# Adaptive-conditioning attention and mixture-of-experts layer: dense units laid into the last batch's head loop, one router for two batches

## What is computed

```python
x = x + attn(wkv(x, f, f, w, u, cond), Wqkv, Wproj)       # 16 heads of 16, q.k scaled by 4
x = x + ffn(wkv(x, f, f, w2, u2, cond))                   # w2, u2: the second pair

# wkv: num and den are two linear recurrences along the tokens, once forwards, once backwards
base = sigmoid(r) * num / max(den, 1e-8);  out = base * (0.8 + 0.2 * tf)

# ffn: 64 experts of width 64 in 8 groups, the 4 best groups, then the 6 best experts of them
h = relu(x @ w1.T) ** 2 * w_dense        # all experts, for all tokens, weighted by the router (mostly 0)
out = h @ w2.T + relu2(x @ shared_up.T) @ shared_down.T
```

## Time and profile before

| | us |
|---|---|
| median of 3 runs (404.63 to 407.39) | 406.7 |
| the profiled execution, its own time | 407.77 |
| its span, first to last instruction | 405.9 |
| PE busy | 317.9 (78%) |
| DVE busy | 322.0 (79%) |
| ACT busy | 201.4 (50%) |
| POOL busy | 126.4 (31%) |
| DMA queue, share of its 16 engines | 50.4% |

### The profile page before, as it was taken

The page is one execution under the profiler, slowest core; times in us unless marked ns, Lnnn a source line. Parts: engine busy times, 40 slices in busy tenths (PEclk is TensorE's granted clock), DMA queues, the critical chain, the costliest instruction groups (busy, mean ns, idle before and its releaser), DMA issues.

```text
span 405.9 us, 6016 instructions
## 1 busy us (share of the span) xinstructions
PE 317.9 (78%) x1552; PEld 245.0 (60%) x1552; DVE 322.0 (79%) x625; ACT 201.4 (50%) x373; POOL 126.4 (31%) x116
## 2 busy tenths in 40 slices
PE   0042378378858887877897897999999999999994
PEld 0031256165737565555665675888888888888882
DVE  6989888966897475686567995888888988888883
ACT  4131406162625264366555564666666666666651
POOL 1519424162050001001222342334334334334331
PEclk9999559658965896896999998999999999999999
DMA  5965907801760176300543544556655566666531
GB/s 174 169 166 151 155 6 185 129 0 56 155 107 3 52 159 103 106 10 8 170 137 131 154 167 156 140 201 186 189 190 192 183 196 190 192 185 190 194 140 52
DMA packets 33055, 55.09 MB, mean 136 GB/s; under 512 B 5207, under 2 KB 13831, under 8 KB 32011
## 3 DMA queue, kind: packets, MB, share of 16 engines
q1 hardware_dynamic: 33034, 54.85, 50.4%
HBM read 47.55 MB, written 5.52 MB: 131 GB/s over the span
## 4 chain that ended last, share of the span: by engine, by line
PE 48%; DVE 13%; issue 3%; ACT 3%; DMA 2%; POOL 1%; DVEq 0%; SPq 0%; ACTq 0%
PE ps L1256 7%; PE ps L1258 7%; PE ps L1257 6%; PE ps L1267 6%; PE ps L1268 6%; PE ps L1269 6%; PE ps L1171 3%; DVE q_st L959 2%; DVE scan L1052 2%; DVE mx L806 2%; PE ps L1139 2%; DMA k_st<-qk_split 2%; DVE qk_lo L1057 1%; PE ps L1158 1%; PE ps L1128 1%
## 5 line engine op out<-in xcount | busy, mean ns | idle before, releaser
L457 POOL TENSOR_TENSOR scan<-scan 128x512 f32<-128x512 f32 x68 | 73.3, 1078 | 137.8 <-ACT scan L584 136.1
L1057 DVE TENSOR_TENSOR qk_lo<-scan,qk_hi 128x512 fp32r<-128x512 f32 x68 | 69.3, 1019 | 31.7 <-ACT qk_hi L591 31.7
L584 ACT ACTIVATE scan<-ps 128x512 f32<-128x512 f32 x68 | 40.7, 599 | 50.2 <-PE ps L1258 50.0
L1267 PE MATMUL ps<-qk_hi,k_st 128*128 128x512 f32 x136 | 54.5, 401 | 4.5 <-DVE qk_lo L1057 4.3
L1256 PE MATMUL ps<-hid_hi,k_st 128*128 128x512 f32 x136 | 54.6, 401 | 2.0 <-DVE q_st L959 2.0
L577 ACT ACTIVATE k_st<-clip 128x512 fp32r<-128x512 f32 x68 | 42.8, 631 | 24.8 <-PE ps L1269 24.8
L1139 PE MATMUL ps<-k_st,q_st 96*128 96x256 f32 x128 | 34.8, 395 | 25.9 <-DMA k_st<-qk_split 22.6
L1258 PE MATMUL ps<-hid_hi,q_st 128*128 128x512 f32 x136 | 54.1, 398 | 0.0
L1257 PE MATMUL ps<-hid_lo,k_st 128*128 128x512 f32 x136 | 53.9, 396 | 0.0
L1268 PE MATMUL ps<-qk_lo,k_st 128*128 128x512 f32 x136 | 53.5, 393 | 0.0
L1269 PE MATMUL ps<-qk_hi,q_st 128*128 128x512 f32 x136 | 53.5, 393 | 0.0
(11 more groups left out here) (118 smaller groups left out, 461.8 us busy)
## 6 DMA issues: line engine op xcount, KB each, us to landing
clip<-in_tiles SPq DMA_DIRECT2D x68, 256.0 KB, 3.0
ex<-gates SPq DMA_DIRECT2D x136, 128.0 KB, 2.9
q_st<-qk_split SPq DMA_DIRECT2D x16, 256.0 KB, 4.8
k_st<-qk_split SPq DMA_DIRECT2D x32, 128.0 KB, 5.6
qk_split<-qk_hi SPq DMA_DIRECT2D x8, 256.0 KB, 2.2
qk_split<-qk_lo SPq DMA_DIRECT2D x8, 256.0 KB, 2.2
f_sb<-in_fT SPq DMA_DIRECT2D x4, 256.0 KB, 10.5
x_sb<-in_xT SPq DMA_DIRECT2D x4, 256.0 KB, 9.7
```

What stands on the lines that cost most here:

```text
L457: g.tensor_tensor(sq[:, k], relu[:, k], relu[:, k], ALU.mult).then_inc(sq_ready, 1)
L1057: TT(act_lo[:, k], act[:, k], act_hi[:, k].bitcast(F32), ALU.subtract).then_inc(act_lo_ready, 1)
L1267: mm(acc, w_hi, act_hi[:, k], start=first, stop=False, skip_group_check=True)
```

## The change

Batch 1's tail is done first, beside the first heads of batch 2. From the second half of batch 2 on there is one loop of 42 slots, s = 0 to 41, on every engine. Slot s holds the shifted scores of one head (batch 2's heads 8 to 15 in slots 0 to 7, batch 3's heads 0 to 7 in slots 9 to 16 and 8 to 15 in slots 18 to 25), the scores of batch 3's head s (slots 0 to 15), and from s=4 on the dense unit n = s-4. The tails of batches 2 and 3 stand in slots 9 to 14 and 27 to 32.

The router handles two batches (512 tokens) at once: 42 steps on tiles twice as wide where the two could be joined, and four small instructions instead of two where they could not. `router(0)` stands alone in slots 0 to 3, six pieces in each; `router(1)` in slots 33 to 36, six pieces in each, beside units. `turn_weights(0)` is in slot 4 before `up(0)`, `turn_weights(1)` in slot 37. On SP the four first weight tiles are loaded before `load_rows(2, 1)`, and `load_rows(3, 0)` and `load_rows(3, 1)` stand behind `load_unit(8)` and `load_unit(16)`.

To make banks free, scores of batch 3 have one PSUM bank instead of two, so do the shifted scores from batch 2's head 8 on, and units 0 to 11 have one bank for `up`. The stacked slot 2 isn't shared with the units' weights any more; the room comes from several buffers that now lie in others (`ekv` in `clip`, `o_ch` in `o_tok`, the router's in `scan` and `num1`). `products` therefore waits for a fourth exponential instead of the third.

```diff
-HEAD = 18
+RT = 2 * QT
+FIRST = 4
+ALONE = 12
+HEAD = NT + RING
@@ banks
         def bank_s(n):
-            return ps[:, n % 2, :].rearrange("p (t k) -> p t k", t=QT)
+            return ps[:, n % 2 if n < H * (B - 1) else 0, :].rearrange("p (t k) -> p t k", t=QT)
 
         def bank_t(n):
-            return ps[:, 2 + n % 2, :].rearrange("p (t q) -> p t q", t=QT)
+            return ps[:, 2 + n % 2 if n < H * (B - 1) - HB else 2, :].rearrange("p (t q) -> p t q", t=QT)
+        def unit_bank(n):
+            return n % 2 if n >= ALONE else 1
@@ SP
+            for b in range(B - 1):
                 load_rows(b, 0)
+                store_qk(b + 1)
+                for w in range(2):
+                    load_stack(w, b + 1, 0)
+                if b == B - 2:
                     sp.wait_ge(ex_ready, 4 * B)
                     sp.wait_ge(esum_ready, 4 * B)
+                    sp.wait_ge(bwd_ready, 8 * B)
                     for n in range(RING):
                         load_raw(n, n)
                 load_rows(b, 1)
+                for w in range(2):
+                    load_stack(w, b + 1, 1)
...
             store_gates(0)
+            for n in range(SHARED, RING):
+                load_spread(0, n, n)
+            for n in range(RING, 9):
+                load_unit(n, 0, n, n % RING)
+            load_rows(B - 1, 0)
+            for n in range(9, 17):
+                load_unit(n, 0, n, n % RING)
+            load_rows(B - 1, 1)
+            for n in range(17, NT):
+                load_unit(n, 0, n, n % RING)
@@ DVE
+            route_now = router(0)
+            for s in range(HEAD + FIRST):
+                n = s - FIRST
+                if s < H:
+                    maximum(3, s)
+                if s < FIRST:
+                    for _ in range(6):
+                        next(route_now, None)
+                if s == FIRST:
+                    route_now = router(1)
+                if s == 8:
+                    low_max(3, 0)
...
+                if s > 32:
+                    for _ in range(6):
+                        next(route_now, None)
+                if n >= 0:
+                    if n > 0:
+                        low_act(n - 1, (n - 1) % 2)
+                    gated(n, n % 2, n % RING, n // RING + 1)
+                    split_lo(n + 2, (n + 2) % RING)
@@ PE
+            for s in range(HEAD + FIRST):
+                n = s - FIRST
+                if s < HB:
+                    shifted_scores(2, HB + s)
+                if HB < s <= 2 * HB:
+                    shifted_scores(3, s - HB - 1)
+                if 2 * HB + 2 <= s < 3 * HB + 2:
+                    shifted_scores(3, s - HB - 2)
+                if s < H:
+                    scores(3, s)
...
+                if s == 4:
+                    turn_weights(0)
...
+                if s == 37:
+                    turn_weights(1)
...
+                if n >= 0:
+                    up(n, n // NT, n % 2, n % RING)
+                if n >= 2:
+                    down(n - 2, (n - 2) // NT, n % 2, (n - 2) % RING, first=(n - 2) % NT == 0, final=n - 2 == NT - 1)
```

More of the change, by code:

```diff
@@ L583, in rectify @@
                     sc.wait_ge(sq_ready, n - 1)
-                a.activation(relu[:, k], bank_h(k), ACT.Relu).then_inc(relu_ready, 1)
+                bank = unit_bank(n) if isinstance(n, int) else k
+                a.activation(relu[:, k], bank_h(bank), ACT.Relu).then_inc(relu_ready, 1)
             def round_act(n, k):
@@ L601, in _ @@
             exponentials(2)
-            for b in range(B):
+            for b in range(2):
                 if b > 0:
@@ new lines, in _ @@
+            low_max(2, 0)
+            maximum(2, HB)
+            maximum(2, HB + 1)
+            normalise(1)
+            maximum(2, HB + 2)
+            maximum(2, HB + 3)
+            split_qk(3, 0)
+            residual(1)
+            maximum(2, HB + 4)
+            maximum(2, HB + 5)
+            split_qk(3, 1)
+            maximum(2, HB + 6)
+            maximum(2, HB + 7)
+            hidden2(1)
+            low_max(2, 1)
+            add_v_bias(3)
+            for n in range(2):
+                split_lo(n, n)
@@ L1310, in _ @@
                 values(b, 1)
-                if b > 1:
-                    turn_weights(b - 2)
-            for h in range(HB + 2, H):
-                shifted_scores(B - 1, h)
-            values(B - 1, 2)
-            values(B - 1, 3)
-            pe.wait_ge(hid_lo_ready, 2)
-            pe.wait_ge(hid_hi_ready, 2)
-            pe.wait_ge(max_ready, H * B)
-            up(0, 0, 0, 0)
-            turn_out(B - 1)
-            up(1, 0, 1, 1)
-            turn_normalised(B - 1)
-            for n in range(2, HEAD):
-                up(n, 0, n % 2, n % RING)
-                if n == 2:
-                    project_out(B - 1)
-                    turn_weights(B - 2)
-                if n == 6:
-                    gate(B - 1)
-                if n == 14:
-                    turn_weights(B - 1)
-                down(n - 2, 0, n % 2, (n - 2) % RING, first=(n == 2))
@@ L1335, in _ @@
-            with pe.Fori(0, (NT - HEAD) // RING) as i:
+            for h in range(HB):
+                shifted_scores(1, HB + h)
+                if h + 2 < HB:
+                    scores(2, h + 2)
+                if h == 4:
+                    values(1, 2)
+                if h == HB - 2:
+                    turn_max(2, 0)
+                    scores(2, HB)
+                    scores(2, HB + 1)
+            values(1, 3)
+            turn_out(1)
+            scores(2, HB + 2)
+            scores(2, HB + 3)
@@ new lines, in _ @@
+            shifted_scores(2, 0)
+            shifted_scores(2, 1)
+            turn_normalised(1)
+            project(3, "q")
+            shifted_scores(2, 2)
+            shifted_scores(2, 3)
+            project_out(1)
+            scores(2, HB + 4)
+            scores(2, HB + 5)
+            project(3, "k")
+            shifted_scores(2, 4)
+            shifted_scores(2, 5)
+            scores(2, HB + 6)
+            scores(2, HB + 7)
+            shifted_scores(2, 6)
+            turn_max(2, 1)
```

592 lines of the change are left out of this document (318 added, 274 removed).

## The result

The changed kernel takes 423.77 us in the median of 4 runs (421.34 to 426.89), beside 406.76 us for the kernel before in the same series: 1.0432 times as long, 95% interval 1.0353 to 1.0511. So the change costs 17 us, where the prediction had 419.0 us, in a range of 405 to 432. The profiled execution took 424.21 us and has a span of 422.4 us, 4.4 more than the 418.0 forecast.

The account below looks back on a forecast made before the run. PE's streaming was taken as the bound. Unit 0 at 172.9 us + 105.2 units + 22.2 other PE work + 25.7 stalls = 326.0 for unit 38; plus 80.3 and 11.7, span 418.0; time 419 us, range 405 to 432.

Parts of the forecast that it names:

- Step 1, the operand: Before unit 0: batch 3's stacked operand lands at 155.1 us, 0.6 us later than in the kernel before.
- Step 1, the rows behind four tiles: Slot 0: the rows of maxima queue behind four weight tiles and land at 159.7 us, 4.0 + 0.6 behind the operand.
- Step 2: Slots 0 to 3: four maxima and all of router(0), 10.4 us, on DVE; unit 0 at 172.9 us, 22.1 sooner.
- Step 3: PE's work from unit 0 to unit 38: 105.2 us of units plus 22.2 of heads, tails and transposes.
- Step 4: PE's stalls from unit 0 to 38, 25.7 us: rows 5.2 and 1.5, tails 2 and 3, router 9.0, clock 5.0.
- Router(1): Slots 33 to 36: DVE needs 19.6 us beside 11.1 of PE, so PE waits 9.0 us (bounds 5 and 17).
- The clock: PE at half clock after three pauses (slots 0 to 3, 9, 37): 5.0 us lost (bounds 0 and 20).
- DVE beside POOL: Second router: DVE slowed by POOL's squares, 2 us counted; the skill's rule alone would add 4.2.
- A: Rival: queue order costs nothing, no waits in slots 0, 9, 18, clock stays up; about 401 us; chance 0.08.
- B: Rival, no change: half of the stalls are in PE's shadow; about 408 us; chance 0.12.
- C: Rival: shared slots run at half clock or bound by hops, +19, 437 us; chance 0.20 together with serialised routers.
- D: Rival: two routers serialise instead of overlapping, at twice a single one each 431 us; chance 0.20 together with half-clock slots.

Follow-up runs that it names:

- experiment 3: The changed kernel with a buffer of its own for `ekv`, so `products` waits for the third exponential again: 421.05 us, ratio 1.0388.
- experiment 4: The kernel before with `products` waiting for the fourth exponential instead of the third: 407.83 us, ratio 1.0078.
- experiment 1: The changed kernel with both `load_rows` of batch 3 issued one unit earlier on SP: 416.65 us, ratio 1.0259.
- experiment 2: The changed kernel with the four first weight tiles issued behind `load_rows(2, 1)` instead of ahead of it: 420.27 us, ratio 1.0366.
- experiment 6: The changed kernel with its routers cut short (no choice of groups and experts, no normalisation): 410.36 us, ratio 1.0171.
- experiment 12: The changed kernel with rows sooner, weight tiles later and `ekv` on its own, a second run of that same kernel: 411.74 us, ratio 1.0094.
- experiment 7: The kernel before with its four routers cut short (no choice of groups and experts, no normalisation): 397.15 us, ratio 0.9834.
- Experiment 10: The changed kernel with rows sooner, tiles later, `ekv` on its own, and also `t_hi` and `t_lo` allocated first: 411.02 us, ratio 1.0097.
- experiment 9: The changed kernel with rows sooner, tiles later, `ekv` on its own, and also its routers cut short: 399.36 us, ratio 0.9865.

## Why the prediction was right, and where its steps were not

The time was 4.8 us above the forecast, and slower was the likely side. The model, unit 0's start plus PE's work plus PE's stalls, held. That the 38 units came within 2.0 us of their sum is in part luck: PE's idle time in them is 14.5 us, where the sum has 20.7, and against that stand half clock, up to 4 us more than forecast, and the pace of the units, 1.3 more. By steps:

**Step 1, the operand: the step that failed.** Forecast 155.1 us, landed at 159.74. Two terms. First, batch 2's loop began 2.7 us later than before (123.91 us against 121.20). Part of this is the later start of `products`, which I had counted at nothing, "DVE scans the other recurrence first": experiments 3 and 4 price it at 1.6 to 3.2 us. Another 0.54 are in that execution's first scan already (9.28 us, before 8.74), and are absent from the profiles of experiments 1, 2 and 6, which have the same front end. How the rest divides can't be told from one profile, as this start varies by 2.4 us between two executions of one program (experiment 12); experiments 1, 2 and 6 have it at 121.8 to 122.2. Second, `evacuate_qk(3, 1)` was to be 0.6 us later for `second_exp(1)`, and was 2.65 us later on top of the above. The chain of after, in that place:

```profile
146.16 0.44 DVE ex L899
146.62 0.63 ACT ex L557
147.25 0.12 ACT den L559
147.68 0.61 ACT ex L561
148.29 0.73 ACT qk_hi L520 x2
149.05 0.89 DVE qk_lo L839 x2
```

and ACT's timeline, with its idle time ahead of the first of the three:

```profile
146.62 0.63 ACT L557 ACTIVATE ex<-ex 128x512 f32<-128x512 f32 x1 [1.80 <-DVE ex L899]
```

The last low part of k starts at 149.05, not 143.70. I had not counted that the first of the three activations waits for DVE's clip, for which ACT stood idle for 1.80 us, and that this clip waits for the output projection: an in-order engine inherits the whole chain of what is put ahead. In the old order that projection came behind this evacuation. Of the 5.35 us, 0.6 were forecast, and with the transfers as before the operand is 4.6 us later than the forecast.

**Step 1, the rows behind four tiles: right in size, in part for another reason.** 4.6 us behind the operand were forecast, 4.1 measured (159.74 to 163.83). DMA issues of after from 155 to 166 us; the last column is the median from issue to landing:

```profile
q_st<-nmax_hi SPq DMA_DIRECT2D x1, 8.0 KB, 5.1
q_st<-nmax_lo SPq DMA_DIRECT2D x1, 8.0 KB, 6.1
```

8 KB take 6.1 us behind the operand and 1 MB of tiles, and 1.9 us in a quiet queue. But behind the operand alone they still take 5.4 (experiment 2), so the tiles lengthen the transfer by 0.7 us only; the larger part is the 3.17 us for which SP was issuing them, which the sum didn't have. Experiment 2 gives 2.7 to 3.5 of the 4.1 back.

**Step 2: right in kind, 1.3 us short.** From the first shifted scores to unit 0 were 13.15 us by the sum and are 14.5. `router(0)` itself took 9.9 us between its first and last step less three maxima (165.70 to 177.39 us on DVE), 0.5 less than 10.4. But its first step came 1.87 us behind the shifted scores, at a clock of 0.50, where the sum had 0.35 and a maximum of 0.6; and from its last step to unit 0 were 0.91 us, the hop and the transpose, for which the sum had nothing. The sentence that router steps between maxima of earlier batches were beside PE's work is doubtful: with all routers cut short (experiment 7) unit 0 of the old order starts 4.6 us sooner, in one profile.

**Step 3: right as far as it can be read,** but for the pace, 2.80 us instead of 2.768. Of the 151.1 us of 38 units, 106.5 are the units at that pace, 14.5 PE's idle time and some 9 the half clock (estimated below); that leaves 21 or a little more for heads, tails and transposes, where 22.2 were forecast. Units 5 to 28 are 3.85 us apart in the mean, single ones 2.8 to 5.6, and not 3.3 to 3.5. Experiment 10 shows the pace to hang on the buffers' places. "Buffers moved into others: off the path" is a second edit wrongly counted at nothing, worth 1.3 us in 38 units and 1.0 in the rest.

**Step 4.** Rows of slots 9 and 18: 5.31 and 1.38 us, forecast 5.2 and 1.5, the best term of the sum, worked out hop by hop from rows of before. Tails: the gate waits are 2.1 us together, of a forecast of 5; no other hop of the tails is among PE's larger waits. Router(1): the size was about right and the place wrong. From unit 28 to unit 33 were 22.1 us for 14.0 us of units, 8.1 lost where 9.0 were forecast. But only 1.22 us of PE's idle time are at `turn_weights(1)`. 3.15 us stand at a `down` whose low part DVE has behind six router pieces, and the rest is half clock and units that drag. The router took 11.0 us of DVE instead of 12.4. The clock: 5.0 forecast; by the windows at 0.82, 0.97 and 0.92 above, PE spent some 9.5, 1.8 and 7.2 us at half clock, an estimate that takes the granted clock as a mean of its two levels. Were PE busy all that time it would lose half of it, 9 us, so 5 was low by up to 4. The half clock lies behind the pauses of 6.58, 5.31 and 3.15 us. The Trainium skill ("TensorE: Matmul & The Clock Gate", HAM oscillation) says that each such wait is paid again with a cold clock, and experiment 1, which removes one, returned more than the wait, in agreement.

**DVE beside POOL.** In the second router two of the small steps are much longer than in the first. Here is one, on DVE, and then POOL's square beside it; in the first router, with POOL idle, that step took 0.23 us.

```profile
301.46 0.94 DVE L948 TENSOR_TENSOR qmax<-scan 128x64 f32<-128x64 f32 x1
```

```profile
301.22 1.10 POOL L469 TENSOR_TENSOR scan<-scan 128x512 f32<-128x512 f32 x1 [1.70 <-ACT scan L603]
```

DVE's step lasts just to POOL's end. L998 is the other, 0.56 us where it was 0.17. It has one SBUF input, so what the prediction cites, on instructions with two, doesn't cover it. These two are 1.1 us, the whole difference between router(1)'s 11.0 and router(0)'s 9.9. I had put 2 for it. The Trainium skill ("SBUF — State Buffer", Who interferes with whom) has one instruction blocked for the length of the other, from which I had estimated 4.2: the trace agrees on the blocked step L948, but of the four squares in that time only two made a step longer; the other two ran beside a reciprocal of 1.75 us and beside the replacement steps of L989, which took as long as in router(0).

**The rivals.** A (queue order free) is refuted by the 5.31 us in slot 9 and by experiments 1 and 2, which gave back 9.7 us together, most of the 11.3 of waits that A left out. B would have needed unit 38 at 315 us; it was at 329.4. C, half clock in the shared slots, came in part: slots 4 to 8 have 0.82, but the slots from 235 us on 1.00. D: the two routers took 9.9 and 11.0 us, not twice a single one, and their extra price over before is about 4 us of 17.

**What the change itself is worth.** Experiments 7 and 9, with the routers cut short and in the second the three faults mended, end within a third of a per cent of each other. The prediction's reason fits this: PE must do heads and units in either order, and it gains only the time in which it idled or ran slowly before. No run tests that reason by itself.

## What to carry to other kernels

When work is put ahead of an instruction on an engine that works in program order, ask what that work itself waits for, and not only how long it takes: here three activations of 1.7 us in all made what stood behind them 2.65 us late. Look in SP's queue for small loads that PE waits on, behind loads that nobody needs yet or that wait themselves; moving them gave 9.7 of 17 us (experiments 1 and 2). And a bubble of half a microsecond wasn't free in a stretch that one engine fills to over 80%: one wait moved by one activation cost 1.6 to 3.2 us (experiments 3 and 4).

## What was not expected of the hardware

The pace of a stream of 512-column matmuls depended on where buffers lie in SBUF: 2.803 us for 12 with `t_hi` and `t_lo` in their later place, 2.775 with them allocated first, 2.770 in the kernel before (units 38 to 67); which buffer counts, and the mechanism, weren't looked for. Issues themselves were long while the operand's 1 MB was on its way: the same six, four tiles and two rows, took SP 4.4 us in after and 4.3 in experiment 2, in either order, with a single one of 1.8 and 1.7 us among them. Two executions of one program had unit 0 at 168.9 and 172.6 us, and in a window from 85 to 92 us one had a granted clock of 0.75, the other 0.50, with 5.9 us of busy PE in both.
